# Reordering the convolution's SBUF buffers and issuing three of the whitening's loads during its last three units

## The reference, cut to what matters

```python
# layer 0: long convolution of every channel with a separable filter (rank 1: hx outer hy)
k = jnp.einsum('ijk,imk->ijmk', hx, hy)[0]          # hx, hy from small sine networks
y = jnp.fft.irfft2(rfft2(x, 2L) * rfft2(k, 2L) / 2L)[..., :L, :L]
x = y + x * bias[:, None, None]
# layer 1: whitening of the channels
x1 = jnp.transpose(x, (1, 0, 2, 3)).reshape(64, -1)
x1_s = x1[:, ::9]
cov = x1_s @ x1_s.T / x1_s.shape[1] + 0.01 * jnp.eye(64)
deconv = _isqrt_newton_schulz(cov, 5)               # (64, 64)
out = deconv @ (x1 - jnp.mean(x1_s, axis=-1, keepdims=True))
```

## Time and profile before

| | us |
|---|---|
| median of 3 runs | 929.42 |
| lowest and highest | 927.54, 931.83 |
| the profiled execution | 929.32 |
| its span in the trace | 927.3 |

### The profile page before, as it was taken

How to read it: one execution, slowest core, us unless ns; L and a number is a source line. 1 busy time by engine, 2 the same in 40 slices (tenths; PEclk the granted TensorE clock), 3 DMA queues, 4 the chain that set the end, 5 groups by cost and what they waited for, 6 DMA issues and landing times.

```text
span 927.3 us, 16068 instructions
## 1 busy us (share of the span) xinstructions
PE 854.4 (92%) x6202; PEld 717.6 (77%) x6202; DVE 578.9 (62%) x640; ACT 400.7 (43%) x716; POOL 494.4 (53%) x278
## 2 busy tenths in 40 slices
PE   2799999999999999999999999998999999877773
PEld 0799999999999999999999999998544444323221
DVE  5398888888888866877768887876333333322221
ACT  2355555555555535555455555551233333222220
POOL 2298888888888866777768877873000000000000
PEclk9999999999999999999999999999999999999997
DMA  3799989989988886999999999997999999999998
GB/s 107 235 319 290 281 288 283 287 286 285 283 284 289 283 279 209 354 344 314 323 321 341 359 342 324 329 325 264 408 394 428 425 427 427 427 427 427 427 428 345
DMA packets 99351, 306.39 MB, mean 330 GB/s; under 512 B 13483, under 2 KB 48332, under 8 KB 84684
## 3 DMA queue, kind: packets, MB, share of 16 engines
q1 hardware_dynamic: 99276, 305.37, 92.4%
HBM read 167.96 MB, written 137.36 MB: 329 GB/s over the span
## 4 chain that ended last, share of the span: by engine, by line
PE 73%; DMA 17%; DVE 3%; SPq 3%; issue 1%; ACT 1%; DVEq 0%; ACTq 0%
PE ps L670 21%; PE ps L782 15%; PE ps L667 12%; PE ps L668 11%; PE ps L669 11%; DMA arena<-convolved 11%; DMA convolved<-arena 4%; PE ps L702 2%; DMA arena<-x 1%; SPq L262 1%; DVE arena L545 1%; SPq L272 1%; SPq L318 1%; DVE arena L505 1%; PE ps L722 0%
## 5 line engine op out<-in xcount | busy, mean ns | idle before, releaser
L670 PE MATMUL ps<-arena 128*128 128x128 f32 x2048 | 394.1, 274 | 0.0
L667 PE MATMUL ps<-rounded 128*128 128x256 f32 x1024 | 373.9, 365 | 10.8 <-DVE rounded L534 8.7
L401 POOL TENSOR_TENSOR arena<-arena,mask 128x1024 f32<-128x1024 f32 x126 | 326.1, 2588 | 68.0 <-DVE arena L545 67.7
L670 PEld LDWEIGHTS ps<-arena 128*128 128x128 f32 x2048 | 315.7, 190 | 0.0
L669 PE MATMUL ps<-rounded 128*128 128x256 f32 x1024 | 288.5, 282 | 0.0
L668 PE MATMUL ps<-rounded 128*128 128x256 f32 x1024 | 288.2, 281 | 0.0
L782 PE MATMUL ps<-arena 128*128 128x512 f32 x488 | 216.3, 597 | 27.9 <-DMA arena<-convolved 27.8
L545 DVE SCALAR_TENSOR_TENSOR arena<-arena,bias_sb,ps 128x1024 f32<-128x1024 f32 x127 | 162.5, 1280 | 91.9 <-DMA convolved<-arena 47.7
L782 PEld LDWEIGHTS ps<-arena 128*128 128x128 f32 x488 | 90.7, 190 | 152.5 <-issue 104.5
L667 PEld LDWEIGHTS ps<-rounded 128*128 128x128 f32 x1024 | 197.0, 192 | 12.1 <-issue 12.0
L367 POOL TENSOR_TENSOR rounded<-arena,rounded 128x512 fp32r<-128x512 f32 x128 | 165.3, 1291 | 72.3 <-ACT rounded L435 70.8
(11 more groups left out here) (93 smaller groups left out, 194.3 us busy)
## 6 DMA issues: line engine op xcount, KB each, us to landing
arena<-x SPq DMA_DIRECT2D x128, 512.0 KB, 5.5
convolved<-arena SPq DMA_DIRECT2D x256, 256.0 KB, 5.4
out<-arena SPq DMA_DIRECT2D x64, 1024.0 KB, 14.6
arena<-convolved SPq DMA_DIRECT2D x47, 1024.0 KB, 18.9
arena<-filters SPq DMA_DIRECT2D x256, 128.0 KB, 4.7
arena<-convolved SPq DMA_DIRECT2D x28, 512.0 KB, 6.2
filters<-arena SPq DMA_DIRECT2D x16, 192.0 KB, 3.5
rounded<-convolved SPq DMA_DIRECT2D x3, 1024.0 KB, 10.7
```

What stands on the lines that cost most here:

```text
L401: nc.gpsimd.tensor_tensor(masked_of(k, 0, PER), by_image(y_sb[k]), mask_of(q // C, 0, PER), ALU.mult).then_inc(masked_done, 1)
L667: mm(wide, hi[:, b, cols], t_hi[k][:, f, :], start=True, stop=False)
L670: last = mm(o[:, b, m * S + P:(m + 1) * S], block1[:, b, cols], t_f32[k][:, f, :], start=False, stop=True)
```

## The change

Three things are changed. The pieces of `rounded` are dealt out anew, and the two x slots of units 123 and 124 get a region of their own (`x_late`) right behind the kept tiles. With that, place 14 is exactly `x_late`, the first place in `rounded` is `x_hi` and `x_lo`, the second holds the filter parts of units 125 and 126, and the third holds the rest. Tile 14 goes to place 14 now, and tiles 15 to 17 to the places in `rounded`. And `load_tile` is called for tiles 14, 15 and 16 inside the loop over the units, each behind a wait of its own: tile 14 behind `store_y(124)`, tile 15 behind `store_y(125)`, tile 16 ahead of `store_y(126)`.

```diff
-        t_hi = [rounded_at(k, S) for k in range(T_SLOTS)]
-        t_lo = [rounded_at(3 + k, S) for k in range(T_SLOTS)]
-        x_hi = [rounded_at(6 + k, S) for k in range(2)]
-        x_lo = [rounded_at(8 + k, S) for k in range(2)]
-        v_hi = [rounded_at(10 + k, S) for k in range(2)]
-        v_lo = [rounded_at(12 + k, S) for k in range(2)]
+        x_hi = [rounded_at(k, S) for k in range(2)]
+        x_lo = [rounded_at(2 + k, S) for k in range(2)]
+        t_hi = [rounded_at(k, S) for k in (6, 10, 4)]
+        t_lo = [rounded_at(k, S) for k in (7, 11, 5)]
+        v_hi = [rounded_at(k, S) for k in (8, 12)]
+        v_lo = [rounded_at(k, S) for k in (9, 13)]
+        x_late = region(2 * XW)
         plain = region(T_SLOTS * 2 * P + 2 * 2 * S + H_SLOTS * 2 * S)
...
-        x_all = region(X_SLOTS * XW)
-        x_sb = [x_all[:, k * XW:(k + 1) * XW] for k in range(X_SLOTS)]
+        x_all = region(3 * XW)
+        x_sb = [x_all[:, k * XW:(k + 1) * XW] for k in range(3)] + [x_late[:, k * XW:(k + 1) * XW] for k in range(2)]
...
-        after_v, after_x, after_y = KEPT + 2, KEPT + 4, KEPT + 5
-        in_at = [*range(KEPT), *range(in_place, resident), *range(KEPT, in_place)]
+        after_v, after_x, after_y = KEPT + 3, KEPT + 4, KEPT + 5
+        in_at = [*range(KEPT + 1), *range(in_place, resident), *range(KEPT + 1, in_place)]
...
             for q in range(UNITS):
                 load_x(q + 4)
+                if q == LAST:
+                    sp.wait_ge(y_mm, LAST)
+                    load_tile(KEPT + 2)
                 store_y(q - 1)
                 load_hankel(q + 5)
                 load_kept(q)
+                if q == LAST - 2:
+                    sp.wait_ge(y_done, LAST - 2)
+                    load_tile(KEPT)
+                if q == LAST - 1:
+                    sp.wait_ge(v_mm, UNITS)
+                    load_tile(KEPT + 1)
...
             sp.wait_ge(y_mm, UNITS)
-            for t in range(KEPT, after_v + READ_ONLY):
+            for t in range(KEPT + READ_ONLY, after_v + READ_ONLY):
                 load_tile(t)
             store_y(LAST)
```

More of the change, by code:

```diff
@@ L305, in _, with load_tile @@
                 load_hankel(q)
+            def load_tile(t):
+                wait(sp, t_stored[out_at[t]], 16 * stores_before_load[t])
+                sp.dma_start(places[in_at[t]], tile_in(t, 0, TW)).then_inc(t_loaded[in_at[t]], 16)
             for q in range(UNITS):
                 load_x(q + 4)
+                if q == LAST:
+                    sp.wait_ge(y_mm, LAST)
+                    load_tile(KEPT + 2)
                 store_y(q - 1)
@@ L311, in _ @@
                 load_kept(q)
-            def load_tile(t):
-                wait(sp, t_stored[out_at[t]], 16 * stores_before_load[t])
-                sp.dma_start(places[in_at[t]], tile_in(t, 0, TW)).then_inc(t_loaded[in_at[t]], 16)
+                if q == LAST - 2:
[4 more added lines that the diff above has]
+                    load_tile(KEPT + 1)
             def store_tile(t):
```

## The result

The changed kernel takes 937.34 us in the median of 5 runs (934.49 to 940.45), the kernel before 929.42 (927.37 to 938.45, 5 runs) beside it: ratio 1.0077, 95% interval 1.0040 to 1.0114. Measured again in e3, on another occasion, with 12 runs against 35: 935.09 to 930.36, ratio 1.0051 (1.0023 to 1.0079). So it is 0.5 to 0.8% slower, where I had forecast 0.4% faster. The profiled execution took 937.3 with a span of 935.5, 8.2 us more than before.

The account below looks back on a forecast made before the run. It took the convolution to end on PE and the whitening to be bound by the DMA engines. Terms -6.1 - 2.3 + 2.0 + 1.0 + 1.6 = -3.8 us gave 925.5 us from 929.32; range 922.6 to 931.0.

Parts of the forecast that it names:

- The leftover goes: -6.1 us: Whitening: the 2.62 MB of earlier loads still unmoved at the first store are gone by then, saving 6.1 us.
- the hole goes: -2.3 us: Early whitening, 668 to 682: SP no longer waits at the first load reusing a place; the rate dip's 2.3 us return.
- supply equals capacity up to tile 32: Whitening: each tile brings 1.4 transfers in 3.44 us, just what the DMA engines move at 427 GB/s.
- My third case, "nothing comes back": Whitening: a shallow queue gives about 357 GB/s, so the gain is refilled and the delay stays: 930.9, chance 0.19.
- +1.6: End of convolution: store 125 lands later behind tile 14's load, delaying the first tile by 1.6 us.
- +2.0: Start of whitening: with an empty queue, two transfers in 6.88 us leave the DMA engines idle for 2.0 us.
- +1.0: Start of whitening: the first store's bytes begin 1.0 us after its issue, no longer hidden by a queue.
- My bound of 2.7: End of convolution: upper limit, 2.7 us, of store 125's delay, with tile 14 loading at 262 GB/s.
- 4.9 us of delay: End of convolution: store 125's delay if tile 14's load took the skill table's 6.15 us; total gain then only 0.5 us.
- The clock: Before the covariance: longer PE idling halves its clock, at most +8.0 us; 934.6 with a 2.7 us delay, chance 0.09.
- I cost the layout at 0: Whole kernel: the new buffer layout moves no instruction and changes no shape, so it costs 0.

Follow-up runs that it names:

- e3: The changed kernel once more, unaltered, on another occasion: 935.09 us, ratio 1.0051 to the kernel before.
- e7: The changed kernel with one load per two stores instead of two per five: 931.43 us, ratio 1.0006 to the kernel before.
- e5: The kernel before with only the two x slots moved, tile 14 fetched there after the convolution's last matmul, and the new tile order: ratio 1.0024.
- e6: The kernel before with one load per two stores instead of two per five, no early loads: ratio 1.0029.
- e9: Against the changed kernel: two early loads only, both behind store 125, x slots in their old place; `rounded` redealt: ratio 1.0005 to the kernel before.
- e13: The kernel before with the x slots moved and the old tile order, no early loads: ratio 1.0014.
- e2: The changed kernel with tile 14 issued behind store 125, so all three early loads follow it: 933.26 us, ratio 1.0033 to the kernel before.
- e4: The kernel before with only the pieces of `rounded` dealt out anew: ratio 1.0002.

## Why the prediction was wrong

**"The leftover goes: -6.1 us" and "the hole goes: -2.3 us".** What these steps say of the queue at the start was nearly right: 2.2 of 2.62 MB of leftover went (5.2 us instead of 6.1), and the first reusing load no longer waited. That the end comes earlier by as much is the step that failed. Forecast was -6.1 - 2.3 + 3.0 = -5.4 us from the first store to the end; the windows show -5.2 - 2.3 + 3.7 at the beginning + 1.4 up to 130 us + 2.3 in the last 20 us = -0.1. The last two terms stood in the sum at nothing. I had written myself that supply equals capacity up to tile 32 and that a queue existing at the start is neither worked off nor grows. The second half is wrong when the queue is short: engines that stand idle with supply at capacity never make it up, and what they did not move becomes queue, so that by tile 25 a store landed after 12.3 us again. And what was left of the head start did not move the end, since some of the engines ended as long after the first store as before. That e7, with a supply above capacity, won 4 us back fits this; why the engines drift apart stays open. My third case, "nothing comes back", was what happened in this stage; I gave it 0.19 and priced it at +1.6. Its mechanism, a rate that depends on the queue's depth alone, is not shown: e5 ran at 422 GB/s from 30 to 100 us after its first store with landings of 14 to 18 us.

**"+2.0" and "+1.0" for the beginning.** The first 30 us moved 20 GB/s less than before, 1.4 us, and that includes the hole that went (2.3 us). So the beginning cost 3.7 against 3.0 forecast.

**"+1.6" for store 125 behind tile 14.** The mechanism is right, the size is 2.3 us in the mean of four profiles against 14, with 1.0 to 3.7 in single ones. My bound of 2.7 was too low. The Trainium skill's 6.15 us for 1 MB alone (DMA: Bandwidth & Descriptors, Bandwidth), from which I had worked out 4.9 us of delay, was above the largest that was seen. Tile 14 took 7.9 us from issue to landing in the changed kernel, with store 124 ahead of it and store 125 behind.

**The clock**, 0.09 in the forecast, fell ahead of the covariance in three of the seven profiles with three early loads, for 1.6 to 2.6 us each, not 8, and in one of the eleven others.

**"I cost the layout at 0"** is likely about 2 us too low, for the x slots; it is not shown by any kernel alone.

Together: nothing back in the whitening, 2.3 us for store 125, some 0.8 us for the clock (the mean of the four kernels with a load ahead less that of the others), and up to 2 us that came with the moved slots make 3 to 5 us, against 4.7 (e3) and 7.2 (first measurement, whose profile also met a late convolution). What of the first measurement lies above 5 us I put down to scatter; it is not shown by itself.

## What to carry to other kernels

Before pricing a freed transfer at its bytes, ask what paces the stage behind it. Here a loop issued just as much as the DMA engines could move, and a head start was not kept. The denser pace alone made the kernel slower (e6), the early loads alone brought nothing (e9) or cost time (e3), and both together only came back to the time of the kernel before (e7). The less SP was held at a place that was not yet free (17.6 us in e6, 0.2 us in e7), the more the denser pace brought. A transfer fetched "in idle time" still stands in a queue: look for the one small store behind it that an engine on the path waits for. And one profile of each kernel can differ by 7 us in a stage that the change does not touch, so compare stages over several kernels before explaining a difference.

## What the runs showed of the hardware

A 256 KB store that lands after 4.4 us in the kernel before took 5.9 to 7.9 us in four profiles with one 1024 KB load issued 2.4 to 3.0 us ahead of it: 1.5 to 3.5 us more, beside 2.5 us for that load's bytes at 427 GB/s. The granted clock fell from 1.00 to 0.50 at the covariance in e13, e2, e3 and e7, where PE had been idle for 2.24, 2.58, 5.00 and 5.51 us, and did not fall in e4 after 2.59 us or in the changed kernel after 2.97 us: the length of the idle time alone does not decide it. At the end of the kernel the DMA share falls from full to nothing over 6 us in one execution and over 9 us in another, with the last store issued 13 us before the end in both.
